# One core, two conditional layers: when the next expert block is turned, and when the next group's first weights are loaded

## The reference

```python
def _L0_cond_ref(x, cat_ids, W, b):                      # W: 64 x 512 x 512
    return jnp.einsum('bsd,bdh->bsh', x, W[cat_ids]) + b[cat_ids][:, None, :]

def _L1_cond_ref(x, indices, fc1_w, fc1_b, fc2_w, fc2_b, experts_w, experts_b):
    h = gelu(jnp.einsum('bnd,hd->bnh', x, fc1_w) + fc1_b)          # exact gelu, h: 2048 wide
    shared = jnp.einsum('bnh,sh->bns', h, fc2_w) + fc2_b           # 384 columns
    expert_x = jnp.einsum('bnh,bph->bnp', h, experts_w[indices]) + experts_b[indices][:, None, :]   # 128 columns
    return jnp.concatenate([shared, expert_x], axis=-1)

x = x + _L0_cond_ref(x, itok_B_0_63, L0_cond_W, L0_cond_b)
x = x + _L1_cond_ref(x, itok_B_0_15, ...)
```

## Time and profile before

| what | value |
|---|---|
| median of three runs | 1680.94 us |
| profiled execution | 1681.4 us, span 1679.6 us |
| TensorE matmul busy | 1639.4 us (98%) |
| TensorE weight loads | 1315.8 us (78%) |
| VectorE busy | 1176.4 us (70%) |
| ScalarE busy | 551.9 us (33%) |
| GpSimd busy | 195.1 us (12%) |
| mean granted TensorE clock | 0.997 |

### The profile page before, as it was taken

The page is one execution under the profiler, slowest core; times in us unless marked ns, Lnnn a source line. Parts: engine busy times, 40 slices in busy tenths (PEclk is TensorE's granted clock), DMA queues, the critical chain, the costliest instruction groups (busy, mean ns, idle before and its releaser), DMA issues.

```text
span 1679.6 us, 28015 instructions
## 1 busy us (share of the span) xinstructions
PE 1639.4 (98%) x7065; PEld 1315.8 (78%) x7065; DVE 1176.4 (70%) x2004; ACT 551.9 (33%) x927; POOL 195.1 (12%) x195
## 2 busy tenths in 40 slices
PE   7899999999999999999999999999999999999999
PEld 5778887877878778787877878778787787878887
DVE  5677667776777767776776677767777677767754
ACT  4343333333323333333332333333333333333321
POOL 0200100111020010200102001110200102001110
PEclk9999999999999999999999999999999999999999
DMA  7886776757677575775767767686775757757630
GB/s 207 185 190 150 147 149 147 156 129 162 127 163 151 131 156 118 167 159 133 149 133 160 156 144 157 131 157 135 163 153 131 155 118 164 163 131 151 134 61 26
DMA packets 884826, 243.44 MB, mean 145 GB/s; under 512 B 803688, under 2 KB 818168, under 8 KB 884732
## 3 DMA queue, kind: packets, MB, share of 16 engines
q1 hardware_dynamic: 740732, 203.75, 57.1%
q10 hardware_dynamic: 144000, 38.82, 10.7%
HBM read 209.93 MB, written 32.51 MB: 144 GB/s over the span
## 4 chain that ended last, share of the span: by engine, by line
PE 66%; SPq 20%; issue 8%; DMA 3%; DVE 2%; ACT 1%; DVEq 0%
PE ps_out L814 30%; PE ps_h L799 14%; PE ps_e L799 13%; PE ps_y L786 8%; SPq L386 8%; SPq L341 4%; SPq L320 2%; DMA e_blocks<-in_L_cond_experts_w 2%; SPq L399 2%; SPq L351 1%; SPq L393 1%; PE ps_t L745 1%; DVE e_whole L643 1%; DVE h L599 1%; DVE w2e L599 1%
## 5 line engine op out<-in xcount | busy, mean ns | idle before, releaser
L814 PE MATMUL ps_out<-w2e,h 128*128 128x512 f32 x3072 | 758.0, 396 | 10.0 <-DVE h L599 10.0
L814 PEld LDWEIGHTS ps_out<-w2e,h 128*128 128x128 f32 x3072 | 574.3, 188 | 152.5 <-DVE h L599 15.9
L799 PE MATMUL ps_e<-y_t,w 128*128 128x512 f32 x1536 | 376.8, 395 | 1.4 <-DVE y_t L599 1.4
L799 PE MATMUL ps_h<-y_t,w 128*128 128x512 f32 x1536 | 375.7, 394 | 0.0
L799 PEld LDWEIGHTS ps_e<-y_t,w 128*128 128x128 f32 x1536 | 290.7, 189 | 66.9 <-DVE y_t L599 1.6
L799 PEld LDWEIGHTS ps_h<-y_t,w 128*128 128x128 f32 x1536 | 288.5, 188 | 65.7
L643 DVE STREAM_TRANSPOSE e_whole<-e_blocks 128x512 f32<-128x512 f32 x256 | 182.0, 711 | 109.3 <-DMA e_blocks<-in_L_cond_experts_w 100.9
L530 ACT CAST w2e<-e_whole 128x512 fp32r<-128x512 f32 x256 | 158.6, 620 | 284.4 <-PE ps_out L814 157.4
L463 POOL TENSOR_TENSOR x_raw<-x_raw,b_all 128x512 f32<-128x512 f32 x60 | 85.3, 1422 | 1354.9 <-DMA x_raw<-in_x 1303.2
L499 ACT CAST w_split<-w_raw 128x512 fp32r<-128x512 f32 x244 | 145.7, 619 | 243.7 <-DMA w_raw<-in_L_cond_W 174.4
L599 DVE TENSOR_TENSOR w_split<-w_raw,w_split 128x512 fp32r<-128x512 f32 x244 | 161.1, 688 | 84.6 <-ACT w_split L499 83.7
(11 more groups left out here) (71 smaller groups left out, 431.3 us busy)
## 6 DMA issues: line engine op xcount, KB each, us to landing
e_blocks<-in_L_cond_experts_w SPq DMA_DIRECT2D x1024, 64.0 KB, 2.9
w_raw<-in_L_cond_W SPq DMA_DIRECT2D x248, 256.0 KB, 2.9
out<-resid SPq DMA_DIRECT2D x64, 256.0 KB, 4.7
x_blocks<-in_x SPq DMA_DIRECT2D x240, 64.0 KB, 2.4
b_all<-in_L_cond_b SPq DMA_DIRECT2D x60, 256.0 KB, 4.3
x_raw<-in_x SPq DMA_DIRECT2D x60, 256.0 KB, 4.6
y_rows<-y ACTq DMA_DIRECT2D x60, 256.0 KB, 2.8
x_blocks<-y_rows ACTq DMA_DIRECT2D x240, 64.0 KB, 3.7
```

The source lines that it names most:

```text
L799: last = nc.tensor.matmul(h_bank(c)[:, :], w1[:, w, k, c * P:(c + 1) * P], y_t[:, a, k, :, :].rearrange("p b s -> p (b s)"), start=(k == 0 ...
L814: last = nc.tensor.matmul(ps_out[b][:, :], h[:, c % 2, a, b * S:(b + 1) * S], fc2_columns(c, c % 2, w, b), start=(c == 0 and n == 0), stop ...
```

## The change

The turn of the next expert block stands behind `h_low` in every step, not only in step 0. The first pair of L0 slices is done in step 2, not in step 1. With it move: its weights, the bias row and x of batch 0 (loaded in step 1, not 0), x_blocks of batch 1 (loaded in step 2, not 1), and the turn of x (in step 1, not 0). The loads of the second pair come in step 2, not 1. On SyncE the store of the previous group stands behind the experts of step 0, not ahead. In group 0 the output-bias loads move to step 1, and the first prep turn stands ahead of `fc1(0, 0)`.

```diff
-    L0_STEPS = (1, 3, 5, 7, 9, 10, 11, 12)
+    L0_STEPS = (2, 3, 5, 7, 9, 10, 11, 12)
...
             def load_l0_in(G, c):
 
-                for b, step in ((0, 0), (1, 1), (2, L0_STEPS[1] + 3), (3, L0_STEPS[3] + 3)):
+                for b, step in ((0, 0), (1, L0_STEPS[0]), (2, L0_STEPS[1] + 3), (3, L0_STEPS[3] + 3)):
                     if c == step:
                         load_x_blocks(G, b)
                 for p in range(2 * GB):
-                    if c == (0 if p == 0 else L0_STEPS[p - 1]):
+                    if c == (L0_STEPS[0] - 1 if p == 0 else L0_STEPS[p - 1]):
...
                 for b in range(GB):
-                    if c == (0 if b == 0 else L0_STEPS[2 * b - 1] + 1):
+                    if c == (L0_STEPS[0] - 1 if b == 0 else L0_STEPS[2 * b - 1] + 1):
                         load_b0(G, b, load_l0_in.cat)
                         load_x(G, b)
...
-                    if c == 0 and not first(g):
-                        store(g - 1)
                     b, quad = (c + 1) % GB, (c + 1) // QUAD + 1
...
-                    if first(g) and c == 0:
+                    if c == 0 and not first(g):
+                        store(g - 1)
+                    if first(g) and c == 1:
                         sp.dma_start(b2_all[:, :], fc2_b.rearrange("(o n) -> o n", o=1).to_broadcast([P, SHARED]))\
...
-                    if c > 0:
-                        turn_next_e(g, c, more)
                     h_high(g, c)
                     prep_low(prep_in_step(g, c, 0))
                     h_low(g, c)
-                    if c == 0:
-                        turn_next_e(g, c, more)
+                    turn_next_e(g, c, more)
                     prep_low(prep_in_step(g, c, 1))
                     if more:
-                        if c == 0:
+                        if c == L0_STEPS[0] - 1:
                             turn_x(g + 1, 0)
...
                 for c in range(NC):
+                    if c == 0:
+                        turn_prep(prep_in_step(g, c, 0))
                     fc1(g, c)
-                    turn_prep(prep_in_step(g, c, 0))
+                    if c > 0:
+                        turn_prep(prep_in_step(g, c, 0))
```

## The result

The changed kernel took 1738.57 us (median of 4 runs, 1736.52 to 1743.38) against 1681.18 us: a ratio of 1.0346, 95% interval 1.0324 to 1.0367. The forecast was 1743 us. The profiled execution has a span of 1736.9 us, 57.3 us more than before.

The account below looks back on a forecast made before the run. TensorE does the work and mostly waits on SyncE's line of DMA issues. Groups 2 to 14 +64, group 1 +2.7, group 0 -5: together +62 us on 1680.9, so 1743 us, range 1714 to 1763.

Parts of the forecast that it names:

- The release: Step 14's late turn frees SyncE's waiting line of loads for the next group later: +3.36 us against TensorE.
- Rival 2: SyncE makes up the 3.36 us, so only its new order counts: +3 us, 1684 us; chance 0.08.
- SyncE's order and the pair's step: Expert DMAs and store ahead of w's issue: +5.84 us, 9.20 in all; TensorE asks for the slices 5.55 us later.
- Rival 3: The first pair gets a whole step of slack and all three waits go: -31 us, 1650 us; chance 0.06.
- The wait in step 2: TensorE stalls before the first pair of L0 slices: 4.65 us in place of 1.00, +3.65 us per group.
- The clock: The longer idle in step 2 makes the granted clock fall in all 13 groups: 2.2 us each, between 0 and 2.8.
- Rival 1: Same as the forecast, but the granted clock doesn't fall: +47 us, 1728 us; chance 0.18.
- Step 3's second wait: Second pair of slices waits for its weights in step 3: 0.7 to 1.25 us, taken as 1.1 at full clock.
- Group 1: Had 2.07 us of slack, so 1.6 us of stall, too short for a clock fall, and 1.1 in step 3: +2.7.
- h: fc2's wait for the low half of h goes once the turn stands behind h_low: -0.93 us per group.
- Sum: Groups 2 to 14: 13 x (3.65 + 2.2 - 0.93) = +64 us.
- Group 0: The 3.4 us stall ahead of a prep transposition and its clock fall (2.8) go: taken as -5, between -6.2 and +1.

Follow-up runs that it names:

- both kernels at 1651 us: Changed kernel with loads where the kernel before had them, plus step 14's turn ahead of h_high (1651.34 us) or quad 1's first batch loaded in step 0 (1651.15 us).
- the release moved: Changed kernel, all turns late, with the first batch of the next group's quad 1 loaded in step 0 instead of step 15: 1671.2 us.

## Why the prediction was right, step by step

The group's own terms, measured on the profile after:
- **The release.** +3.28 us (3.36 forecast). Rival 2, that SyncE makes it up, is out: 11.77 against 11.76 us from the turn to x_blocks, and the late turn alone costs 48 us.
- **SyncE's order and the pair's step.** w at +9.16 us (9.20), and the demand 5.55 later. Rival 3 needed less than 4.6 us of shift.
- **The wait in step 2.** Over groups 2 to 14 the time from the start of the last fc2 matmul to that of the first slice is longer than a matmul's slot by 57.9 us, before by 11.7: +3.55 us per group (3.65).
- **The clock.** 13 falls in 13 groups. From the first slice on TensorE worked 51.4 us at the lower level, half of which is 25.7, or 2.0 per group (2.2). Rival 1 is out. It was an extrapolation from one gap of 3.4 us, and held here. One reading under it was wrong: of the idle times up to 1.6 us the prediction says that none was followed by a fall, but the lower stretch at 36.7 starts 0.7 us behind the end of an idle time of 1.40 us (timeline of TensorE, kernel before):
```profile
33.97 0.66 PE L745 MATMUL ps_y<-ident,y 128*128 128x128 f32 x4 [0.79 <-DVE y L634]
36.03 4.61 PE L799 MATMUL ps_e<-y_t,w 128*128 128x512 f32 x12 [1.40 <-DVE y_t L599]
```
The waits of 3.6 us and more didn't put that to the test.
- **Step 3's second wait.** Covered by the slow clock as written. With the clock up it is there. Group 1 of the changed kernel, whose clock stayed, loses 1.26 us in step 3 (1.1 forecast). With step 14's turn early it is 0.3 to 1.2 us in eleven of 13 groups, next to nothing in two.
- **h.** The wait is gone; fc2 has no wait for it in the table. Before, fc2 lost 13.4 us in groups 2 to 14, 1.03 per group (0.93).
- **Sum.** From gelu(0) of group 2 to that of group 15 the kernel takes 57.1 us more, 4.39 per group; forecast 4.92. The terms, 3.55 + 2.0 - 1.03, make 4.5; the last 0.1 is not traced. Group 1 takes +3.1 (+2.7).
- **Group 0** was mis-sized: -2.9 us, forecast -5. The 3.4 us stall is gone as said, but the prep turns now wait in other places (2.0, 1.7 and 1.4 us at 44, 60 and 84 us of the trace). And the 2.8 us of the fall did not come: group 0 has two stretches at the lower clock, as before, at 35.0 and 45.2 us, 10.2 us long in both kernels. That the late turn is what helps there, the other runs bear out: all nine with late turns are 1.7 to 6.4 us faster than the kernel before in group 0, the one with all turns early is 1.4 us slower. This miss of +2 partly cancels the 7 us by which groups 2 to 14 were put too high, which is how 62 became 57.3; that the forecast came so near is in part luck.

What the profile of the changed kernel was to show came in each point. The experiments add what the prediction couldn't: once SyncE isn't held up by step 14's turn, the loss is gone but for some 2 us at most, whichever of the two ways that is done (1684.95 and 1671.2 us). The store's new place on SyncE was never changed by itself; both kernels at 1651 us have it.

## What to carry to other kernels

Before an instruction is moved later on its engine, list who waits for its semaphore, DMA queues above all: a queue that issues in order and has no slack carries the delay to everything behind it, here through a loop's branch and into the next group. A demand moved later is no slack if the transfer that feeds it is moved behind other issues by as much. A wait in which TensorE stands still costs more than its length once it is long enough for the granted clock to fall: filling it with useless matmuls was cheaper than the idle time.

## What the runs showed of the hardware that I had not expected

The granted clock can fall after shorter idle times than the 3.4 us of the kernel before. In the changed kernel with all turns early it fell in two groups, both after waits of 2.0 us (timeline of TensorE, then the window):
```profile
482.29 1.74 PE L786 MATMUL ps_y<-w_split,x_t 128*128 128x512 f32 x6 [1.99 <-DVE x_t L599]
483.82 4.46 PE L799 MATMUL ps_h<-y_t,w 128*128 128x512 f32 x12
```
```profile
483.70:487.10 3.40, 3.40 (x10) 2.66 (x9) 2.76 (x3) 0.00 (x0) 3.11 (x3) 0.50 0.65 94
```
In the run with the extra matmuls it fell twice, after waits of 1.76 and 1.78 us, but not after one of 2.06, nor after one of 2.35:
```profile
806.33 2.64 PE L783 MATMUL ps_y<-w_split,x_t 128*128 128x512 f32 x6 [1.76 <-DVE x_t L599]
...
1123.00 2.00 PE L783 MATMUL ps_y<-w_split,x_t 128*128 128x512 f32 x6 [1.78 <-DVE x_t L599]
```
```profile
595.99 1.63 PE L783 MATMUL ps_y<-w_split,x_t 128*128 128x512 f32 x6 [2.06 <-DVE x_t L599]
```
In the run with loads early and all turns late, eleven waits of 1.5 to 2.3 us stand in step 3, and the clock stays after every one. Its longest:
```profile
484.88 1.65 PE L783 MATMUL ps_y<-w_split,x_t 128*128 128x512 f32 x6 [2.30 <-DVE w_split L599]
```
With the release moved, one of 2.31 us brought a fall. So up to 2.35 us the length of the wait alone doesn't decide (in group 0 of the kernel before a fall stands behind one of 1.40 us), while above 3.5 us all 26 waits in groups 2 to 14 (13 in the changed kernel, 13 with the late turn alone) brought a fall. What decides in between was not tried.
